# A four-block recurrent kernel: the last period's second layer four steps sooner, decays in halves after the recurrence, and five output banks

## What is computed

```python
x = x + L0(x)   # every level of the Haar transform is multiplied by one gate: x * (1 + gate), so x * (2 + gate) in all
x = x + L1(x)   # h_t = tanh(x_t @ Wx + b + h_{t-1} @ Wh), a recurrence over 512 steps
x = x + L2(x)   # f, i = sigmoid(x @ Wf + bf), sigmoid(x @ Wi + bi); c = x @ Wc + bc
                # fn, in = f / (f + i), i / (f + i); lr = log(fn + 1e-8)
                # hidden_t = cumsum_t(exp(sum(lr) - cumsum(lr)_{t-1}) * in * c) + exp(cumsum(lr)_t) * h0
x = x + L3(x)   # out = x @ (base + A B^T) with a factor pair A, B of rank 8 for each sequence
```

## Time and profile before

| | |
|---|---|
| median of 3 runs | 1496.57 us (1495.63 to 1499.19) |
| profiled execution, its own time | 1498.06 us |
| its span, first to last instruction | 1496.1 us |
| mean granted TensorE clock | 0.977 |
| busy: PE, PEld | 1422.0 us (95%), 1124.8 us (75%) |
| busy: DVE, ACT, POOL | 1006.8 us (67%), 659.6 us (44%), 682.1 us (46%) |
| DMA moved | 168.15 MB |

### The profile page before, as it was taken

The page is one execution under the profiler, slowest core; times in us unless marked ns, Lnnn a source line. Parts: engine busy times, 40 slices in busy tenths (PEclk is TensorE's granted clock), DMA queues, the critical chain, the costliest instruction groups (busy, mean ns, idle before and its releaser), DMA issues.

```text
span 1496.1 us, 49921 instructions
## 1 busy us (share of the span) xinstructions
PE 1422.0 (95%) x21159; PEld 1124.8 (75%) x21159; DVE 1006.8 (67%) x2707; ACT 659.6 (44%) x2185; POOL 682.1 (46%) x536
## 2 busy tenths in 40 slices
PE   6789999999999999999999999999997996999998
PEld 4457888888888888888888888888886874677776
DVE  4333757575757576767676666666656689898884
ACT  3444444545454545444444444444444442233332
POOL 2422444444444444434353535343424355777773
PEclk9799999999999999999999999999997997999999
DMA  9660142423232323333333323242315457888893
GB/s 351 225 245 18 33 84 41 76 49 68 52 65 52 66 51 66 58 59 58 59 61 62 64 54 67 53 70 52 58 31 107 113 112 139 284 316 308 315 329 124
DMA packets 441904, 168.15 MB, mean 112 GB/s; under 512 B 406433, under 2 KB 409633, under 8 KB 438354
## 3 DMA queue, kind: packets, MB, share of 16 engines
q1 hardware_dynamic: 441682, 164.97, 43.6%
HBM read 96.78 MB, written 68.16 MB: 110 GB/s over the span
## 4 chain that ended last, share of the span: by engine, by line
PE 90%; DVE 3%; issue 2%; ACT 2%; POOL 1%; DMA 1%; SPq 0%; ACTq 0%; DVEq 0%; POOLq 0%
PE bank L466 47%; PE recb L432 28%; PE bank L627 12%; PE bank L641 1%; PE bank L513 1%; DMA xt<-in_Wx 1%; ACT gates L813 1%; PE recb L610 1%; PE spare L610 1%; PE aux L478 1%; DVE pre L1150 0%; DVE pre L1148 0%; DVE hs L1155 0%; DVE pout L1214 0%; ACT hs L652 0%
## 5 line engine op out<-in xcount | busy, mean ns | idle before, releaser
L432 PEld LDWEIGHTS recb<-hs,scanS 128*128 128x128 f16 x16384 | 444.7, 96 | 172.6 <-DVE hs L1155 169.8
L432 PE MATMUL recb<-hs,scanS 128*128 128x32 f16 x16384 | 495.3, 177 | 25.9 <-DVE hs L1155 25.9
L652 ACT ACTIVATE hs<-pre 128x64 f16<-128x64 f32 x512 | 131.6, 257 | 621.6 <-DVE pre L1150 620.1
L1148 DVE TENSOR_TENSOR pre<-recb,xw 128x64 f32<-128x64 f32 x512 | 114.9, 224 | 266.6 <-PE recb L432 262.8
L1016 DVE RECIPROCAL gates<-gates 128x64 f32<-128x64 f32 (+1 forms) x484 | 258.1, 554 | 0.4
L1155 DVE TENSOR_TENSOR hs<-konst,hs 128x64 f16<-128x64 f32 x512 | 115.0, 225 | 137.0 <-ACT konst L653 137.0
L875 POOL TENSOR_TENSOR xt<-xt,hbuf 128x512 f32<-128x512 f32 (+1 forms) x65 | 98.8, 1520 | 177.7 <-ACT hbuf L656 177.7
L863 POOL TENSOR_TENSOR x1lo<-xt,x1hi 128x512 fp32r<-128x512 f32 x62 | 80.6, 1301 | 198.8 <-ACT x1hi L662 198.8
L881 POOL TENSOR_TENSOR gates<-gates 128x512 f32<-128x512 f32 x64 | 83.0, 1296 | 165.4 <-DVE gates L1016 165.4
L890 POOL TENSOR_TENSOR xt<-xt,pout 128x512 f32<-128x512 f32 x64 | 76.2, 1191 | 149.6 <-DVE pout L1042 144.5
L1150 DVE TENSOR_TENSOR pre<-recb,pre 128x64 f32<-128x64 f32 x512 | 114.8, 224 | 17.6
(11 more groups left out here) (202 smaller groups left out, 2730.4 us busy)
## 6 DMA issues: line engine op xcount, KB each, us to landing
xt<-in_x SPq DMA_DIRECT2D x64, 256.0 KB, 3.5
g_d<-gst SPq DMA_DIRECT2D x64, 256.0 KB, 3.8
n_d<-nst SPq DMA_DIRECT2D x64, 256.0 KB, 3.1
x_d<-xt SPq DMA_DIRECT2D x64, 256.0 KB, 3.1
out<-gates SPq DMA_DIRECT2D x64, 256.0 KB, 6.5
xt<-x_d SPq DMA_DIRECT2D x28, 512.0 KB, 4.6
stage<-in_w SPq DMA_DIRECT2D x11, 1024.0 KB, 5.8
xt<-g_d SPq DMA_DIRECT2D x14, 512.0 KB, 6.9
```

The costliest lines, as they stand in the source:

```text
L432: last = nc.tensor.matmul(rec[:, m].rearrange("p a b -> p (a b)"), w[:, k, m * P:(m + 1) * P], hs[:, k].rearrange("p a b -> p (a b)"), sta ...
L652: nc.scalar.activation(hs[:, :, 0, :], pre[t % 2][:], ACT.Tanh, scale=unscale).then_inc(s_h, 1)
L1148: nc.vector.tensor_tensor(pre0[:], rec[:, :, 0, :], xw[j % 2][:, t], ALU.add).then_inc(s_pre0, 1)
```

## The change

The diff, cut to its core. Lines of the kernel after it are some 25 to 45 higher than before.

```diff
+AHEAD = 4
+
+def moved_up(table, kinds):
+    out = {}
+    for t, items in table.items():
+        for item in items:
+            if t < CARRIED:
+                out.setdefault(t, []).append((t, item))
+            if item[0] not in kinds and t >= CARRIED:
+                out.setdefault(t, []).append((t, item))
+            elif item[0] in kinds:
+                at = (t if t >= CARRIED else t + TS) - AHEAD
+                if at < TS:
+                    out.setdefault(at, []).append((at + AHEAD, item))
+    return out
+
+ACT_LAST = moved_up(ACT_WORK, "fig")
+DVE_EARLY_LAST, DVE_LATE_LAST = (moved_up(t, ("x1", "s", "r", "n", "p", "k")) for t in (DVE_EARLY, DVE_LATE))
...
-        yp = [s[:, 0:P] for s in (recb, spare)]
+        yp = [recb[:, 0:P], turned]
+        obank = bank + [spare]
+
+        def quarter(b, t):
+            return obank[(NT * b + t) % len(obank)]
...
-                        if GROUPS[n][0] != "x" or j + 1 < NBLK:
-                            group_part(n, lo, lo + 1, j)
+                    if j + 1 < NBLK:
+                        for e in range(t * QUOTA, (t + 1) * QUOTA):
+                            group_part(e // GM, e % GM, e % GM + 1, j)
+                    else:
+                        for e in range(max(C * GM, (t + AHEAD) * QUOTA), min(len(GROUPS) * GM, (t + AHEAD + 1) * QUOTA)):
+                            group_part(e // GM, e % GM, e % GM + 1, j)
...
                 for t in range(NT):
-                    if m == 0 and b:
-                        pe.wait_ge(s_o, NT * (b - 1) + t + 1)
+                    if m == 0 and NT * b + t == len(bank):
+                        pe.wait_ge(s_P, 2 * C * NBLK)
+                    elif m == 0 and b:
+                        pe.wait_ge(s_o, NT * b + t - len(bank))
...
-                        last = nc.tensor.matmul(bank[t][:], x3[q][:, m, tok], w[:, m, :], start=(m == 0 and e == 0), stop=False)
+                        last = nc.tensor.matmul(quarter(b, t)[:], x3[q][:, m, tok], w[:, m, :], start=(m == 0 and e == 0), stop=False)
...
             last = NBLK - 1
-            for m in range(C // 2):
-                x2_low(last, m)
-            shares(last - 1, 3)
             add_P(last - 1, 1)
+            add_P(last - 1, 2)
             shares(last, 0)
-            add_P(last - 1, 2)
             add_P(last - 1, 3)
...
-            def whole_decay(b, m):
...
+            def decays(b, m, first=0):
+                for h in range(first, 2):
+                    carry(b, m, h)
+                    decay(b, m, h)
...
-            recip(last - 1, 3, 6)
-            recip(last - 1, 3, 7)
-            dve.wait_ge(s_x2, C * NBLK)
-            nc.vector.memset(seeds, 0.0).then_inc(s_zero, 1)
-            dve.wait_ge(s_zero, 3)
-            for m in range(C // 2, C):
+            for m in range(C):
                 dve.wait_ge(s_x2h, C * last + m + 1)
                 nc.vector.tensor_tensor(x2lo[:, m, :], xt[3][:, m, :], x2hi[:, m, :].bitcast(F32), ALU.subtract).then_inc(s_lowd, 1)
-            new_info(last - 1, 2, GROUPS.index(("c", 2)))
-            whole_decay(last - 1, 1)
-            new_info(last - 1, 3, GROUPS.index(("c", 3)))
-            whole_decay(last - 1, 2)
+            decays(last - 1, 1, 1)
+            decays(last - 1, 2)
             shares_of(0)
-            whole_decay(last - 1, 3)
+            decays(last - 1, 3)
```

## The result

| | before | changed kernel |
|---|---|---|
| median of the runs | 1499.45 us (9 runs, 1495.63 to 1505.20) | 1492.27 us (9 runs, 1484.38 to 1493.91) |
| ratio, 95% interval | | 0.9929 [0.9910, 0.9948] |
| profiled execution | 1498.06 us | 1486.2 us |
| its span | 1496.1 us | 1484.3 us |

The change makes the kernel faster by 0.7%, 10.6 us by the ratio (7.8 to 13.5). I had forecast 15.8 us and 1480.8 us, range 1476.5 to 1487.5. The direction was right; the median lies outside the range. Both profiled executions of the table have the shorter one.

The account below looks back on a forecast made before the run. The prediction took PE as the bound, DVE and DMA not far behind, and DVE's list between recurrence and first batch. Terms 10.8 + 4.0 + 1.7 - 0.9 + 0.2 = 15.8 us gave 1480.8 us, range 1476.5 to 1487.5.

Parts of the forecast that it names:

- Five banks: Batch loop: PE no longer waits for ACT's copy of quarter 0; 0.77 us at 14 boundaries, 10.8 us saved.
- DVE's 1.32 us shrink to 0.55: Batch loop: DVE's idle time before y_low was slack that covers the 0.77 us gained per boundary.
- first rival: Batch loop: loads come late, the period stays 13.79 us, time 1491.6 us; 12%, half of it likelier than all.
- Half decays: Behind the recurrence: five decays as two halves in PSUM take 10.5 us instead of 14.5, saving 4.0 us on DVE.
- the new wait: Behind the recurrence: DVE waits 0.45 us for the gates of chunks 2 and 3 each, costing 0.9 us.
- The list ahead of the first sum: Start of block 15's second layer: the first sum of gates starts 1.7 us sooner, bounds 0.4 and 3.2.
- The last period: Recurrence's last period: the first two of the last four steps may be 0.1 us shorter, 0.2 us saved.
- the 13.0 of "right": Batch loop: the forecast would be confirmed, among other signs, by batches 13.0 us apart.
- the 13.4 of "wrong": Batch loop: the forecast would be refuted if batches stayed above 13.4 us with DVE or a DMA named.
- From the profiled execution's own 1498.06: Whole time: subtracting the summed 15.8 us from the old kernel's profiled execution gives 1482.3 us.
- The median of the runs is 1.5 us lower: Whole time: the median lies 1.5 us below the profiled execution, turning 1482.3 into the forecast 1480.8 us.

Follow-up runs that it names:

- whole_decays: Changed kernel with the six decays behind the recurrence as one scan each from seeds in SBUF, as before; ratio 0.9933, 274.51 us from the last difference.
- no_sooner: Kernel before with only the five banks and the half decays, without the last period's work begun four steps sooner; 1490.99 us, ratio 0.9909.
- filler: Changed kernel with 6 idle matmuls in each of the last four steps and 6 behind the last one; ratio 0.9912.
- after_again: The changed kernel run once more without any edit, to see how well stretches repeat; 1492.48 us.
- banks_alone: Kernel before with the fifth output bank alone, factor products of odd batches moved to make room; ratio 0.9957.
- both: Changed kernel with ACT casting y_high ahead of the cast that waits for DVE, plus idle matmuls in and behind the last four steps; ratio 0.9888.
- all_four: Kernel of both, with DVE's y_low(0) moved behind the first sum of batch 1 and 10 idle matmuls between batches 0 and 1; 1482.80 us, ratio 0.9877.
- four_banks: Changed kernel with four output banks as before, everything else of the change kept; ratio 0.9961.

## Why the prediction was wrong

Two steps failed: the term for the five banks, and the step from one profiled execution to a median. The mechanism of the first is shown by runs; the cause of the second is open.

**The sum.** From the last difference to the end the change saves 283.14 - 270.87 = 12.3 us, and in the last period 0.2. Forecast were 15.8. One term accounts for the difference but for some tenths.

*Five banks, 10.8 us forecast, 7.0 measured.* The wait of PE went as foretold, 0.77 a boundary. The step that failed is the sentence "DVE's 1.32 us shrink to 0.55". I took DVE's idle time before `y_low` for slack that ends with PE's factor products, and did not look at what stood ahead of `y_high` in ACT's queue. There it was the cast of DVE's own last addition, so that 0.85 us of the 1.32 were no slack. 12.47 + 0.85 = 13.32 us is a floor under the batch, 0.47 below the old period and not 0.77. The trace of before had the number, in batch 1, on DVE and on ACT:

```profile
1294.99 0.69 DVE L1195 TENSOR_TENSOR xt<-xt,aux 128x512 f32<-128x512 f32 x1
1296.53 0.29 DVE L1199 TENSOR_TENSOR x2hi<-spare,x2hi 128x128 fp32r<-128x128 f32 x1 [0.85 <-ACT x2hi L807]
```

```profile
1295.71 0.62 ACT L799 CAST wf_hi<-xt 128x512 fp32r<-128x512 f32 x1 [2.43 <-DVE xt L1195]
1296.24 0.26 ACT L807 CAST x2hi<-spare 128x128 fp32r<-128x128 f32 x1
```

PE's factor products there began at 1293.13 and lasted 1.07 us, so `y_high` could have started at 1294.2; it started 2 us later, behind the cast of DVE's addition.

My first rival, batches fed no faster, named DVE and the loads among its reasons and thought half of it likelier than all. It came to 0.3 of 0.77 in every batch, by a mechanism that I had not named. What the Trainium skill's page "TensorE: Matmul & The Clock Gate" (section "HAM oscillation — how this bites in real kernels") reports of its own kernel, that PSUM double-buffering gave no further gain, does not carry over to this one, where PE's wait was for ACT's copies: here a fifth bank gave 7.0 us.

*Half decays, 4.0 forecast, and the new wait, -0.9.* The 3.6 us of whole_decays are the two terms together, for 3.1 forecast. From the first sum of gates to the last information DVE took 41.18 us before and 37.66 after, 3.52 less. The wait is there, ahead of the sums of chunks 2 and 3 as foretold, but 0.77 us each, 1.54 in all. So the list itself became 5.1 us shorter: both terms were too small, in opposite directions. The durations were right: 0.17 + 0.70 wherever GpSimd was. The section "1. Specifications" of the page "GPSIMD Engine Reference" in the Trainium skill says that GpSimd's SBUF interfaces are shared with VectorE, and contended for by VectorE instructions with two SBUF inputs. The rows agree: the scan with its seeds in SBUF took 1.26 us with GpSimd idle and 2.31 beside it, the one with seeds in PSUM 0.70 for half the columns in both cases (in the changed kernel at 1217.62 with GpSimd idle and at 1228.78 beside it).

*The list ahead of the first sum, 1.7 forecast.* From the last difference to the sum it was 11.55 us before, and 11.04 and 9.81 in the two traces of the changed kernel: 0.5 or 1.7. But no_sooner has 10.10 with the old order, so that most of such a gain comes with the halves alone. I had seen that the clock would be at 0.50 and priced it at 1.3 to 2.7 us; filler shows 2.5 where the clock fell late. So the size was within my bounds. What I missed is the comparison: the clock was up before and need not have fallen, so that the four steps, taken by themselves, give back what they gain.

*The last period, 0.2 forecast,* 74.18 us before and 73.99 after from one block's last difference to the next. That is not clear of scatter: whole_decays, with the same last period as the changed kernel, took 74.22 and after_again 74.85.

Without the banks the change gave 276.12 - 270.87 = 5.25 us from the last difference to the end, with 4.0 + 1.7 - 0.9 = 4.8 forecast. That is partly luck. Up to the last information it gave 4.0 (0.51 + 5.06 - 1.54); the other 1.2 came behind it, where I had no term. There DVE's wait for the factor products of batch 0 fell from 2.76 to 2.22 us, a gap of 0.48 in its list went away, and the batches up to the last addition took 194.99 us for 195.34.

Of the signs that I had named, the wait of PE is gone, the halves last what I said and the waits for chunks 2 and 3 are there. The period of 13.32 us lies between the 13.0 of "right" and the 13.4 of "wrong", and the last information came 4.0 us sooner, not about 5.

**The absolute time.** The step that failed is "From the profiled execution's own 1498.06" with "The median of the runs is 1.5 us lower": it takes the recurrence to last equally long in every execution. I counted from a profiled execution of the shorter kind, and all three runs of the table before were near it (median 1496.57); the nine runs of the result have 1499.45. Of the changed kernel's nine runs two (1484.38 and 1486.20) are inside my range and seven, from 1491.79 on, lie 5.6 us or more above those two. With 7.0 in place of 10.8 for the banks the forecast would have been 1484.6: right for the shorter kind, and still 7.7 us below the median. A range moved up by the same 3.8 us would have ended at 1491.3, below the median too. By their times the seven are of the longer kind; of the changed kernel only after_again, at 1492.48 us, has a trace that shows it. What it is that picks the kind I have not found. The range's lower end does not come out of its own terms either: 1480.8 less 2.0 for the decays and 1.5 for the clock is 1477.3, not 1476.5; this changed nothing.

## What to carry to other kernels

When a wait of the bounding engine is to be removed, take the next engine's idle time apart before calling it slack: follow its releaser back through that engine's queue, and see whether the work ahead of it depends on the waiting engine itself. Such a loop, here 0.85 us, is a fixed part of the period as long as the order stays. And when matmuls are moved out of the end of a phase, look at what TensorE does next and at which clock; work that only keeps it busy can be worth more than the work that was saved. Where a change is small against the scatter of whole runs, compare stretches between landmarks that every version has.

## What was unexpected of the hardware

The recurrence has two periods with the same instructions. The changed kernel's differences at the start of blocks 8 and 9 (counted from 0), in its first trace and in after_again:

```profile
631.06 0.23 DVE L1199 TENSOR_TENSOR hs<-konst,hs 128x64 f16<-128x64 f32 x1
704.02 0.22 DVE L1199 TENSOR_TENSOR hs<-konst,hs 128x64 f16<-128x64 f32 x1
```

```profile
633.62 0.23 DVE L1199 TENSOR_TENSOR hs<-konst,hs 128x64 f16<-128x64 f32 x1
707.00 0.22 DVE L1199 TENSOR_TENSOR hs<-konst,hs 128x64 f16<-128x64 f32 x1
```

72.96 against 73.38 us. In each of twelve profiled executions every block from 3 to 14 is within 0.02 us of one of the two: six have the shorter (before, changed kernel, banks_alone, whole_decays, both, all_four), six the longer. Around 800 us steps alternate between 2.26 and 2.30 us in the changed kernel's first trace, which is of the shorter kind; in four_banks, of the longer, each takes 2.29. From 800 to 820 us the granted clock is 1.00 in both, and the instructions of a step last equally long (matmuls 177 ns, tanh 257, difference 225). It looks as if a step could lock in at either of two phases between DVE and PE, but no run tested that.

The granted clock of TensorE fell and rose at different distances from the same place of the program in two traces of one kernel. In the first it averaged 0.55 over 1210 to 1215 us and 0.93 over 1220 to 1225 (windows above): at 0.50 from about 2.9 us before the last difference until 7.3 behind it. In after_again, where that difference is at 1219.81:

```profile
1211.00:1215.00 4.00, 2.07 (x66) 1.73 (x64) 2.88 (x9) 0.69 (x4) 1.18 (x1) 0.90 1.01 356
1215.00:1220.00 5.00, 2.07 (x64) 1.86 (x64) 2.88 (x11) 1.54 (x10) 2.54 (x3) 0.50 0.50 112
1220.00:1225.00 5.00, 3.58 (x10) 2.88 (x11) 4.65 (x11) 2.66 (x5) 0.81 (x2) 0.55 0.33 56
```

By the same working it was at 0.50 from 5.6 us before until 4.7 behind. As long a time at 0.50 thus held fewer of the gates' products, and the first sum of gates came 1.2 us sooner.

It came to nothing, because in batch 0 the clock rose later. The windows behind the last information, first trace and after_again:

```profile
1263.00:1267.00 4.00, 3.62 (x15) 2.65 (x15) 3.63 (x5) 1.19 (x5) 3.68 (x3) 1.00 0.48 75
1268.00:1272.00 4.00, 3.97 (x9) 3.15 (x10) 3.63 (x4) 1.29 (x5) 3.64 (x3) 0.50 0.88 158
```

PE made 15 matmuls in the one and 9 in the other, and its factor products of batch 0 started 56.6 and 56.5 us behind the last difference. DVE, which was 1.2 us sooner in after_again, waited 3.41 us for them in place of 2.22.
